# Routing logits computed with tokens as rows, instead of experts as rows and a transpose

## The reference

```python
x = x + attn(layernorm(x), Wq, bq, Wk, bk, Wv, bv)        # 16 heads of 16, 4 key groups, causal
x = x + xattn(layernorm(x), ctx, ctx, Wc, bc)             # the same heads against a context
x = x + ffn(layernorm(x), gate_weight, Wg, Wu, Wd, Sg, Su, Sd)

# inside ffn, x of shape (4096, 256):
logits = x @ gate_weight.T                                # (4096, 64)
scores = softmax(logits)
# the best 3 of 8 groups of experts by their largest score, then the best 6 experts in them
topk_w, topk_i = top_k(where(group mask, scores, 0), 6)
# each expert takes its first 95 tokens and one more: silu(x Wg) * (x Wu), then Wd
y = sum over the 6 of topk_w * expert output
shared = silu(x @ Sg.T) * (x @ Su.T) @ Sd.T
return y + shared
```

## Time and profile before

| | |
|---|---|
| median of 3 runs | 725.83 us (722.03 to 725.87) |
| the profiled execution | 728.12 us, of which the span of instructions is 726.4 |
| TensorE busy | 651.5 us, 90% of the span |
| VectorE busy | 452.0 us, 62% |
| ScalarE busy | 336.1 us, 46% |
| GpSimd busy | 340.1 us, 47% |
| TensorE busy between 250 and 300 us | 45.37 of 50 us |
| VectorE busy between 250 and 300 us | 45.04 of 50 us |
| the logits' products (line 499) | 32 instructions, 15.4 us busy |
| the logits' transposes (line 507) | 32 instructions, 3.7 us busy |
| the copy between them (line 684) | 8 instructions, 579 ns each |

### The profile page before, as it was taken

One profiled execution on the slowest core, in us unless ns is written; L12 is line 12 of the kernel. 1 busy time (PEld: TensorE's weight loads), 2 busy tenths in 40 slices (PEclk: granted clock), 3 DMA queues, 4 the chain that ended last, 5 costly groups with the idle time before them and its releaser, 6 DMA issues. The chain is left out here.

```text
span 726.4 us, 16967 instructions
## 1 busy us (share of the span) xinstructions
PE 651.5 (90%) x6417; PEld 467.9 (64%) x6417; DVE 452.0 (62%) x1147; ACT 336.1 (46%) x639; POOL 340.1 (47%) x378
## 2 busy tenths in 40 slices
PE   3899999999879998899989899999999986899993
PEld 1466666667667776667764455687887864678562
DVE  6476766678868889898974799533334322234293
ACT  3677777767658767766654423222222211122000
POOL 5222122213524434444322555676666777765462
PEclk9999999999989999999999999999999999999976
DMA  8233443265463223222311430278999987795795
GB/s 252 45 58 85 87 90 77 44 106 107 106 107 72 60 53 80 72 51 44 98 37 44 137 110 0 53 206 236 256 252 269 241 218 187 194 244 88 185 364 174
DMA packets 111616, 94.27 MB, mean 130 GB/s; under 512 B 59248, under 2 KB 95344, under 8 KB 111536
## 3 DMA queue, kind: packets, MB, share of 16 engines
q1 hardware_dynamic: 96368, 74.57, 39.4%
q0 software_dynamic: 10368, 14.30, 10.4%
q10 hardware_dynamic: 4800, 4.33, 1.8%
HBM read 60.26 MB, written 24.50 MB: 117 GB/s over the span
## 5 line engine op out<-in xcount | busy, mean ns | idle before, releaser
L1454 POOL DMA_INDIRECT sum_d<-outs,targets x64 | 92.1, 1439 | 40.0 <-issue 16.8
L1534 DVE TENSOR_TENSOR hid<-sil,Sc 88x192 f32<-88x192 f32 x64 | 22.4, 350 | 133.2 <-issue 76.2
L1279 PE MATMUL Sc<-xT,wgu_sb 128*88 128x96 f32 x1024 | 96.6, 248 | 1.9 <-issue 1.9
L795 DVE TENSOR_REDUCE mx<-Sc 128x16 f32<-128x1024 f32 x64 | 78.2, 1223 | 28.1 <-PE Sc L434 27.9
L1279 PEld LDWEIGHTS Sc<-xT,wgu_sb 128*88 128x88 f32 x1024 | 90.6, 158 | 2.6 <-issue 2.3
L658 ACT COPY ET<-ring 128x512 f32<-128x512 f32 x128 | 68.8, 589 | 40.6 <-PE ring L446 37.9
L462 PEld LDWEIGHTS O<-vbd,ET 128*64 128x64 f32 x2048 | 66.5, 138 | 29.4 <-issue 16.9
L799 DVE TENSOR_TENSOR E<-Sc,mx 128x1024 f32<-128x1024 f32 x64 | 78.4, 1225 | 6.9 <-DVE mx L795 0.5
L446 PE MATMUL ring<-ident,E 128*128 128x128 f32 x512 | 69.5, 279 | 12.3 <-ACT E L697 12.3
L462 PE MATMUL O<-vbd,ET 128*64 128x34 f32 x2048 | 73.6, 225 | 3.6 <-ACT ET L658 3.0
L434 PE MATMUL Sc<-kbd,qT 64*64 64x256 f32 x1024 | 72.5, 386 | 4.7 <-DMA kbd<-kT 4.7
(11 more groups left out here) (203 smaller groups left out, 1175.5 us busy)
## 6 DMA issues: line engine op xcount, KB each, us to landing
wgu_sb<-in_wgu_dram SPq DMA_DIRECT2D x64, 352.0 KB
wd_sb<-in_wd_dram SPq DMA_DIRECT2D x64, 176.0 KB
sum_d<-zeros SPq DMA_DIRECT2D x16, 524.0 KB, 6.1
kbd<-kT SPq DMA_DIRECT2D x248, 32.0 KB, 2.2
X<-in_x_dram SPq DMA_DIRECT2D x8, 512.0 KB, 7.4
rows_d<-xhT SPq DMA_DIRECT2D x8, 512.0 KB, 3.0
xnT<-sum_d SPq DMA_DIRECT2D x8, 512.0 KB, 9.5
out_dram<-X ACTq DMA_DIRECT2D x8, 512.0 KB, 4.4
```

The costliest lines, as they stand in the source:

```text
L795: nc.vector.reduce_max(mx[:, m % 2, :], sc, AX.X).then_inc(s_mx, 1)
L1279: last = nc.tensor.matmul(GP[e % 2][0:MH, CAP * u:CAP * (u + 1)], wgu[:, j, 4 * MH * c + MH * u:4 * MH * c + MH * (u + 1)], xT[:, e % 2, c ...
L1454: pool.indirect_dma_start(w["sums"][e % 2], bass.IndirectOffsetOnAxis(ap=targets[:, e:e + 1], axis=0), outs[:, e % EB, :], None, compute_o ...
```

## The change

The logits are computed with the tokens as rows at once. The transposed rows in `xnT` become the stationary side, 128 tokens at a time, and the gate matrix moves with its 64 columns. The product stands at m%4 = 1, in the place of the transposes `logits_t`, and writes the bank that VectorE reads. The product at m%4 = 0, ScalarE's copy, the buffer `logT` and the ring's use `LP` are gone.

```diff
@@ ring_uses, m % 4 == 0
-            if routed((m - 8) // 4):
-                uses.append((("LP", (m - 8) // 4), "act"))
@@ TensorE
             def logits(g):
-                out = empty_bank(("LP", g))
+                out = empty_bank(("LT", g))
                 pe.wait_ge(*saved(("XN1", g)))
-                for c in range(2):
-                    last = nc.tensor.matmul(out[0:NE, :], gate[:, c, :], xnT[:, c, TOK * (g - NG):TOK * (g - NG + 1)],
-                                            start=c == 0, stop=c == 1)
-                last.then_inc(s_fill, 1)
-
-            def logits_t(g):
-                out = empty_bank(("LT", g))
-                pe.wait_ge(*saved(("LP", g)))
                 for t in range(GT):
-                    last = nc.tensor.transpose(out[:, NE * t:NE * (t + 1)], logT[:, 128 * t:128 * (t + 1)],
-                                               ident[0:NE, 0:NE])
+                    at = TOK * (g - NG) + 128 * t
+                    for c in range(2):
+                        last = nc.tensor.matmul(out[:, NE * t:NE * (t + 1)], xnT[:, c, at:at + 128], gate[:, c, :],
+                                                start=c == 0, stop=c == 1)
                 last.then_inc(s_fill, 1)
@@ TensorE, m % 4 == 1
-                        logits_t((m - 9) // 4)
+                        logits((m - 9) // 4)
@@ TensorE, m % 4 == 0
-                    if routed((m - 8) // 4):
-                        logits((m - 8) // 4)
@@ ScalarE
-            def logits(g):
-                name = ("LP", g)
-                act.wait_ge(s_fill, ring.filled(name))
-                if g >= NG + 1:
-                    act.wait_ge(s_fill, ring.filled(("LT", g - 1)))
-                nc.scalar.copy(logT[:], bank(name)[0:NE, :]).then_inc(s_act, 1)
```

More of the change, by code:

```diff
@@ L214, in attention_phase @@
     Sc, O, banks = mem["Sc"], mem["O"], mem["ring"]
-    xnT, gate, desc, pack, logT, lg, m4, r4, sc, gs, gs2, g8, gm, tmp, tmp2, t8, wa, rmv, rst, rrstd, rnmr = (
-        mem[k] for k in ("xnT", "gate", "desc", "pack", "logT", "lg", "m4", "r4", "sc", "gs", "gs2", "g8", "gm", "tmp",
+    xnT, gate, desc, pack, lg, m4, r4, sc, gs, gs2, g8, gm, tmp, tmp2, t8, wa, rmv, rst, rrstd, rnmr = (
+        mem[k] for k in ("xnT", "gate", "desc", "pack", "lg", "m4", "r4", "sc", "gs", "gs2", "g8", "gm", "tmp",
                          "tmp2", "t8", "wa", "rmv", "rst", "rrstd", "rnmr"))
@@ L1730, in decoder_layer @@
         stack.append(attn)
-        for name, shape in (("gate", [128, 2, NE]), ("desc", [128, NB]), ("pack", [128, 128 // BT]), ("logT", [NE, TOK]), ("lg", [128, GT, NE]),
+        for name, shape in (("gate", [128, 2, NE]), ("desc", [128, NB]), ("pack", [128, 128 // BT]), ("lg", [128, GT, NE]),
                             ("m4", [128, GT]), ("r4", [128, GT]), ("sc", [128, GT, NE]), ("gs", [128, GT * NGRP]),
```

## The result

The changed kernel is faster, by more than was forecast. Twenty executions of each gave medians of 718.63 us after and 724.12 before. The ratio of the means, each without its slowest execution, is 0.994 with a 95% interval of 0.992 to 0.9961. The base's own median over these twenty, in which the three that I had seen are included, is 1.7 us lower than over the three.

A forecast was written before the change was run, and what follows sets the result against it. VectorE was taken to set the pace in the middle attention groups and TensorE in the tail. Gains of 0.3 (group 0), 0.2 (group 4) and 0.54 us (tail) made 1.1 us: 725.83 to 724.7 us, range 720.6 to 728.3.

The forecast's parts named there:

- The pair's price: New logical products on TensorE: one 128-column load with its 64-column matmul costs 0.115 us, sixteen in a group 1.84 us.
- The cheap case: Rival: a new pair costs only 0.061 us, like line 507's transposes; 3.8 us gained, 722.0 us; chance 0.22.
- the unhidden case: Rival: loads not hidden beside matmuls, 0.190 us a pair, 731.2 us (at 0.16, 727.0); chance 0.12.
- Groups 1 to 3: Middle attention groups: gain 0, VectorE's timeline unchanged, TensorE's wait for the residual add grows from 0.41 to about 0.7 us.
- Group 4: Attention group where VectorE's row maximum waits 0.22 us for scores: that wait goes, gain 0.2 us.
- Group 0: First routed attention group: VectorE's 1.41 us wait goes, the next step's TensorE work is 1.44 us longer; gain 0.3 us.
- the ring: Bank ring loses one use per group; probabilities' transposes then wait for a residual add instead of a copy, priced at nothing.
- the removed term: TensorE at step m%4 = 0: four 512-column instructions at 0.43 us pitch go, 1.71 us a group.
- the tail: Groups 6 and 7, where TensorE's run is the chain: 0.27 us each, gain 0.54 us.
- the 0.27 of my balance: TensorE per group: 1.71 us and 0.40 us removed, 1.84 us added, 0.27 us less.
- the forecast case: The prediction's own case: 1.1 us gained, 724.7 us, likeliest between 724.0 and 725.5; chance 0.60.
- The clock rival: Rival: a microsecond's shift moves clock falls at 206 or 410 us, 3.4 us either way, 728.1 or 721.3; chance 0.06.

The follow-up runs named there:

- x8: Changed kernel with each group's sixteen new load-and-matmul pairs issued twice; 729.48 us, tile 41's maximum to the barrier 184.27 us against 171.09.
- x7: Kernel before with the gate matrix padded by 64 zero columns to 128; 722.59 us, tile 41's maximum to the barrier 172.92 us against 173.56.
- x6: Change made for groups 0 to 5 only, old product, copy and transposes for the others; 719.98 us, tile 41's maximum to the barrier 172.45 us.
- x3: Kernel before with the expert stage replaced by a store of the residual rows; median 427.81 us.
- x5: Change made for the last two routed groups only, groups 0 to 5 as before; 723.12 us, tile 41's maximum to the barrier 173.79 us.
- x12: Kernel before with the expert stage replaced by a store of the residual rows, more executions; median 424.12 us.
- x14: Kernel before with the expert stage replaced by a store of the residual rows, more executions; median 424.33 us.
- x9: Changed kernel again, no new edit, for the size of the whole effect; median 719.63 us, ratio 0.9938.
- x4: Changed kernel with the expert stage replaced by a store of the residual rows; median 423.67 us.
- x13: Changed kernel with the expert stage replaced by a store of the residual rows, more executions; median 423.12 us.
- x15: Changed kernel with the expert stage replaced by a store of the residual rows, more executions; median 423.06 us.

## Why the prediction was right and wrong

**Right.** The pair's price: 0.115 us was forecast, (392.41 - 390.59) / 16 = 0.114 measured, with the way to the next block in it. The cheap case (0.061) and the unhidden case (0.16 or 0.19) are both gone: all rows are loaded and all are in use, and the pair costs less than the load alone lasts. Groups 1 to 3: no gain, and the wait behind the logits grew, to 0.78 us where I said about 0.7. x8 showed that this wait is a cover of about that depth. Group 4: 0.2 forecast, 0.27 to 0.29 found. Group 0: 0.3 forecast, 0.47 found; the wait of 1.41 us went, and most of it came back as the longer step behind it. No new wait came from the ring.

Two rules of the Trainium skill's page "TensorE: Matmul & The Clock Gate" can be held against the 0.114 us. That of the section "LDWEIGHTS (loading the stationary operand)" gives 0.107 for 128 columns, an estimate, and the trace is close to it. That of the section "The mechanism", by which a load overlaps running matmuls only with other row groups, does not hold for these pairs.

**Wrong: the removed term.** "Four are 1.71 us" counted the matmuls and not the block's edges. In the tail the three pitches of 1.81, 1.86 and 1.89 us hold 0.40 us more than three times 1.72, and all of it went with the block and its transposes. x7 shows the two edges at the block, for it took them away and kept the products: 0.64 us over groups 6 and 7, 0.32 a group. The third, before the transposes, is the 0.09 that x7 left. With the 0.27 of my balance this is 0.68 of the 0.71 us a group that both groups show. The tail gave 1.42 us instead of 0.54. I had read the pitch from twenty products of like shape in a row, where no edge occurs, and had not read the rows at the block's own ends, though the bracket of the transposes' load, [0.79 <-issue], stands in the earlier trace rows.

**Wrong: a place left out.** 0.31 us were gained between tile 63's maximum and its probabilities' transposes, which I had counted as VectorE's pace. The timelines suggest ScalarE: the transposes of tile 62 start 0.65 us ahead of tile 63's maximum instead of 0.30, so ScalarE's copies are done earlier, and the exponential behind them too. This link was only read, not tried. x6 has this gain without the tail's change (41.31 against 41.62 us from tile 63 to the barrier).

**Wrong: the time.** Of about 4 us measured, 1.1 were forecast, 1.4 more are these two mistakes and the small excess in groups 0 and 4, and 1.3 to 1.7 stay open (the whole effect of 3.8 at an equal clock, or of 4.2 as it is, less the 2.5 of the stretch). The absolute time missed the range by 2 us, because the base moved by 1.7 and the effect was larger. The bound of half a per cent was passed by a hair (0.6%), where I gave 0.20. The range let the forecast case scatter by too little: I saw 722.0 to 725.9 in three executions of before, and twenty of them cover 717.6 to 733.8.

**What stays open.** Whether some 1.5 us more are gained outside the stretch. The attention stage alone, at equal clock, points to half of that before tile 41 or in the clock's falls, which one profile a kernel can't settle. The lower clock behind tile 63's wait was in four of eight profiles with the old groups before it (x3, x5, x12, x14) and in two of nine with the new ones (x8, x9); that may be chance. One of the nine, x4, had a fall behind the weights' transposes of a middle group, whose wait the change lengthened to 0.78 us; its stretch is 2.4 us longer than those of x13 and x15. One profile can't tell whether the longer wait brought it.

The clock rival, by which a shift of a microsecond moves such falls, was right in kind: falls of 1.6 us come and go in profiles of the same kernel. No run shows that the change moved them.

## What to carry to other kernels

Price a block of products by the time from its first instruction to the first of the next block, in the very place where it stands, and not by the pitch inside a long run: where products with a 64-column stationary side stood between products with 96 or 128 columns, and before transposes with 64 rows, each edge cost 0.09 us or more here, 0.40 us for three. Where TensorE is the chain, try products of like load shape side by side, even if it means loading zeros; here that was worth 0.64 us in the one profile taken. And before counting work that goes away, look which engine ends the waits around it: the same saving was worth 0.71 us in the tail and nothing in three groups of the middle.

## What was not expected of the hardware

- The load of 64 columns behind products of 128, and the load of 96 behind products of 64, were not started ahead of the running matmuls: nothing was loaded for 0.76 and 0.81 us before them. With 128 columns in place of the 64 both were started ahead, after 0.24 us, the load of 96 behind those of 128 too. Padding 64 columns to 128 made the load longer (0.137 to 0.190 us) and the kernel's stretch 0.64 us shorter.
- A pair of a 128-column float32 load and a 64-column matmul has a pitch of 0.114 us, less than the 0.192 us that its load alone lasts: loads and matmuls on all rows run beside each other.
- Behind the same wait of 1.70 to 1.74 us the clock stayed at its upper level in some executions and fell to the lower in others (6 of 17 profiles), at a price of 1.6 us.
